# A fused attention kernel: the value products of a tile in two halves, at two places

## The reference

```
scores = jnp.einsum('bhid,bhjd->bhij', q, k) * scale
attn = jax.nn.softmax(scores + causal_mask, axis=-1)
y_softmax = jnp.einsum('bhij,bhjd->bhid', attn, v)
```

## Time and profile before

| | |
|---|---|
| median of 3 runs | 2063.31 us |
| the profiled execution, its time and its span | 2065.87 us, 2064.1 us |
| PE, DVE, ACT, POOL busy, of the span | 88%, 76%, 67%, 56% |
| first stage, attention, third stage (by the places where value products begin and end) | 279, 1610, 175 us |
| value products' matmul records (line 1179) | 2816 + 1792, two for each f32 matmul |
| mean granted clock of TensorE | 0.931 |

### The profile page before, as it was taken

How to read it: one execution, slowest core, us unless ns; L and a number is a source line. 1 busy time by engine, 2 the same in 40 slices (tenths; PEclk the granted TensorE clock), 3 DMA queues, 4 the chain that set the end, 5 groups by cost and what they waited for, 6 DMA issues and landing times. The chain is left out here.

```text
span 2064.1 us, 47119 instructions
## 1 busy us (share of the span) xinstructions
PE 1811.0 (88%) x15280; PEld 706.0 (34%) x15280; DVE 1559.0 (76%) x1712; ACT 1384.5 (67%) x2853; POOL 1147.8 (56%) x1130
## 2 busy tenths in 40 slices
PE   5995589999999899999989999999999999986733
PEld 3452123333334333333343333333333333322622
DVE  5433888888888788887888888888888888501867
ACT  2442158888877788888767888887677887864221
POOL 3102266666666566666665675756576767600535
PEclk9996579999999999999999999999999999997865
DMA  4878131223122312322124214122322121102601
GB/s 127 185 186 208 36 91 57 73 60 85 59 64 78 85 58 85 74 77 66 52 74 95 73 55 99 51 63 68 84 70 84 54 62 59 34 6 74 179 7 75
DMA packets 144582, 163.60 MB, mean 79 GB/s; under 512 B 63440, under 2 KB 91088, under 8 KB 144336
## 3 DMA queue, kind: packets, MB, share of 16 engines
q1 hardware_dynamic: 141952, 158.74, 28.6%
q10 hardware_dynamic: 2384, 1.77, 0.3%
HBM read 122.00 MB, written 38.01 MB: 78 GB/s over the span
## 5 line engine op out<-in xcount | busy, mean ns | idle before, releaser
L1327 DVE TENSOR_REDUCE pmax<-PS 128x2 f32<-128x1024 f32 (+3 forms) x1152 | 1251.1, 1131 | 219.7 <-PE PS L1124 185.1
L1277 ACT ACTIVATE probs<-PS 128x512 f32<-128x512 f32 (+3 forms) x2304 | 1126.5, 567 | 321.6 <-PE PS L1158 231.7
L1158 PE MATMUL PS<-Q_st,K_st 50*128 50x512 f16 (+3 forms) x1408 | 414.8, 363 | 30.2 <-ACT probs L1277 13.6
L1042 POOL TENSOR_TENSOR v_exp<-v_exp,k_rows 128x512 f32<-128x512 f32 x256 | 319.9, 1274 | 64.2 <-DMA v_exp<-qkv_t 63.8
L1124 PE MATMUL PS<-K_st,Q_st 48*128 48x512 f16 (+3 forms) x1408 | 349.7, 360 | 5.3 <-DVE pmax L1327 4.8
L1179 PE MATMUL PS<-probs,V_g 128*17 128x512 f32 (+3 forms) x2816 | 342.8, 560 | 0.0
L1158 PE MATMUL PS<-Q_st,K_first 50*128 50x512 f16 (+3 forms) x896 | 275.4, 382 | 20.2 <-issue 7.2
L1124 PE MATMUL PS<-K_first,Q_st 48*128 48x512 f16 (+2 forms) x896 | 239.8, 413 | 52.1 <-DVE pmax L1327 37.1
L1075 POOL TENSOR_TENSOR state<-ends,q_rows 128x516 f32<-128x516 f32 x256 | 276.1, 1111 | 0.0
L1070 POOL COPY carry<-ends 128x4 f32<-128x4 f32 x64 | 12.1, 189 | 469.4 <-DVE ends L1362 469.4
L1158 PEld LDWEIGHTS PS<-Q_st,K_st 50*128 50x128 f16 x1408 | 110.4, 94 | 406.4 <-ACT probs L1277 326.5
(11 more groups left out here) (163 smaller groups left out, 1584.5 us busy)
## 6 DMA issues: line engine op xcount, KB each, us to landing
v_exp<-qkv_t SPq DMA_DIRECT2D x256, 256.0 KB
qkv_t<-proj SPq DMA_DIRECT2D x24, 512.0 KB, 3.7
qk_parts<-parts SPq DMA_DIRECT2D x16, 512.0 KB, 5.3
Q_st<-qk_parts SPq DMA_DIRECT2D x192, 32.0 KB, 3.4
v_rows<-vaug SPq DMA_DIRECT2D x32, 136.0 KB, 6.6
xin<-x SPq DMA_DIRECT2D x8, 512.0 KB, 6.5
k_rows<-qkv_t SPq DMA_DIRECT2D x16, 256.0 KB, 4.0
q_rows<-qkv_t SPq DMA_DIRECT2D x16, 256.0 KB, 5.0
```

Of the source, the lines that this page charges most:

```text
L1042: pool.tensor_tensor(v_exp[:, n % RING], v_exp[:, n % RING], k_rows[:, b % 2], ALU.mult)\
L1158: mm = pe.matmul(PS[:, bank, 0:CH - r * P], keys[rows, pair, kt * P:(kt + 1) * P], Q_st[rows, c, pair, r * P:CH], start=True, stop=(kt < T ...
L1277: act.activation(probs[:, tile % P_SLOTS, h, 0:CH - r * P], PS[:, step[5], 0:CH - r * P], ACT.Exp, scale=SCORE_SCALE).then_inc(exp_done, 1)
L1327: dve.tensor_reduce(pmax[:, s % 2, pair * TPC + j:GH * TPC:PAIRS * TPC, blk], PS[:, bank:bank + SIDES, 0:width], AX.X, ALU.max).then_inc(m ...
```

## The change

`TILE_ORDER` becomes "SUMMvSSMMRSV". Where the value products of the tile before stood last, with all their columns, there are now two steps: `v` behind the first pair of maxima does columns 0 to 255 of the output (part 0), and `V` at the end does columns 256 to 511 (part 1). The waits (on `exp_done`, and at a chunk's first tile on `out_evacuated` and the values' load) stand before part 0; `values_done` is counted at the end of part 1. Where the mask leaves part 0 no columns (r of 2 or 3), part 0 issues no matmul, only its waits. `PAIR` is 256.

```diff
-TILE_ORDER = "SUMMSSMMRSV"
+TILE_ORDER = "SUMMvSSMMRSV"
...
-    def values():
-        s, kt = pending.pop(0)
-        steps.append(("values", 0, s, kt))
+    def values(part):
+        s, kt = pending[0]
+        steps.append(("values", 0, s, kt, part))
+        if part == 0:
+            return
+        pending.pop(0)
...
-                elif kind == "V":
+                elif kind in "vV":
                     if pending:
-                        values()
+                        values("vV".index(kind))
...
-    values()
+    values(0)
+    values(1)
...
+                        first, end = max(r * P, part * PAIR), (part + 1) * PAIR
+                        if part == 0:
+                            if kt == 0:
+
+                                pe.wait_ge(out_evacuated, g * NCH + s + 1)
+                                if s in FIRST_USE:
+
+                                    pe.wait_ge(loaded["v_" + FIRST_USE[s]], g * 16 + 16)
+
+                            pe.wait_ge(exp_done, g * GH * TILES + GH * (tile + 1) + GH * TILES)
+                        if first >= end:
+                            return
                         for h in range(GH):
-                            mm = pe.matmul(PS[h * VW:h * VW + VN, O_BANK, r * P:CH], v[:, kt, h * VN:(h + 1) * VN],
-                                           probs[:, tile % P_SLOTS, h, 0:CH - r * P],
-                                           start=(kt == 0), stop=(kt == KEY_TILES[s] - 1))
-                        mm.then_inc(values_done, 1)
+                            mm = pe.matmul(PS[h * VW:h * VW + VN, O_BANK, first:end], v[:, kt, h * VN:(h + 1) * VN],
+                                           probs[:, tile % P_SLOTS, h, first - r * P:end - r * P],
+                                           start=(kt == 0 and part == 0), stop=(kt == KEY_TILES[s] - 1))
+                        if part == 1:
+                            mm.then_inc(values_done, 1)
```

More of the change, by code:

```diff
@@ L1162, in scores, with values @@
                         mm.then_inc(scores_ready, 1)
-                    def values(g, s, kt):
+                    def values(g, s, kt, part):
                         c = ORDER[s]
@@ L1168, in values @@
                         r = max(kt - TPC * c, 0)
[L1169 to L1174, removed]
                         v = V_first if s < FIRST_USERS and kt < FIRST * TPC else V_g
-                        pe.wait_ge(exp_done, g * GH * TILES + GH * (tile + 1) + GH * TILES)
-                        for h in range(GH):
-                            mm = pe.matmul(PS[h * VW:h * VW + VN, O_BANK, r * P:CH], v[:, kt, h * VN:(h + 1) * VN],
-                                           probs[:, tile % P_SLOTS, h, 0:CH - r * P],
-                                           start=(kt == 0), stop=(kt == KEY_TILES[s] - 1))
-                        mm.then_inc(values_done, 1)
+                        first, end = max(r * P, part * PAIR), (part + 1) * PAIR
[7 more added lines that the diff above has]
+                            return
+                        for h in range(GH):
+                            mm = pe.matmul(PS[h * VW:h * VW + VN, O_BANK, first:end], v[:, kt, h * VN:(h + 1) * VN],
[3 more added lines that the diff above has]
+                            mm.then_inc(values_done, 1)
                     def lag(g, b, part, bank):
@@ L1230, in walk @@
                             elif kind == "values":
-                                values(g, s, step[3])
+                                values(g, s, step[3], step[4])
                             elif kind == "burst":
```

## The result

The changed kernel takes 2151.66 us (median of 4 runs, 2149.99 to 2154.97) against 2067.19 us (4 runs) before: a ratio of 1.041, with a 95% interval of 1.0372 to 1.0448. It is slower by about 84 us; 2155 us and a ratio of 1.044 had been forecast. The spans of the two profiled executions are 2064.1 and 2149.1 us.

The account below looks back on a forecast made before the run. A plain tile was bound by a ScalarE loop of 2.37 us, becoming 2.60 through v. Terms 48 + 11 + 6 + 5 + 21 = 91 us gave 2154, stated as 2155 us (+4.4%), range 2095 to 2190, likeliest case 2125 to 2190.

Parts of the forecast that it names:

- What bounds the kernel now: Plain attention tile: a loop through ScalarE (S0, its exponential, S3, value products, next S0) of 2.37 us closes the 2.38.
- The wait that moves: Plain tile: v waits for the previous tile's fourth exponential with S1, S2, S3 behind it; new loop 2.60 us, chance 0.78.
- plain tiles: Tiles without burst, lag, turn or mask: +0.22 us each, 48 us in three groups, and 11 us in the last.
- PE's own sum: PE's work in a plain tile, without waits, rises by 0.46 to 2.45 us.
- The rival in which PE alone bounds: Plain tiles: no wait in front of v, 2.45 us a tile or less, 2111 us in all; chance 0.09.
- The split at +0.14: Value products on PE: two halves cost 1.12 us where one whole took 0.98.
- The sum of 91 us: Whole kernel: the added terms, 48 + 11 + 6 + 5 + 21 us.
- masked tiles and chunk beginnings: The four tiles at each of 28 chunk boundaries: 0.75 us a chunk, 21 us, with ends of -11 and +52.
- bursts: 16 a group, set by PE: +0.09 us each, 6 us over 64.
- lags and turns: Some 23 tiles a group where an output's turn adds PE work between V and S0: 0.05 us each, 5 us.
- The halves that help: Rival, plain tiles: shorter V brings S0 0.42 us earlier, ScalarE's idle time goes, tile falls to 2.28, 2026 us; chance 0.06.
- The clock: Rival: PE stalls in every tile drop the clock; one tile in ten at half speed adds 140 us, 2295; chance 0.04.

Follow-up runs that it names:

- the control: The kernel before, value products whole and last in the tile, but taken from the tile two before: 2068.92 us, ratio 1.0005.
- the wait alone: The changed kernel with the waits kept at v's place but no matmul there, all 512 columns at the tile's end: 2072.3 us, ratio 1.0016.
- the halves at the end: The changed kernel with v directly in front of V at the tile's end: 2075.98 us, ratio 1.0018.
- the later tile: The changed kernel with both halves taken from the tile two before instead of the tile before: 2092.26 us, ratio 1.0103.
- v behind S1 and S2: The changed kernel with v two places later, behind score products S1 and S2: 2108.03 us, ratio 1.0184.
- the whole early: The kernel before with its whole value products, 512 columns unsplit, moved to v's place: 2339.24 us, ratio 1.1296.
- the cuts at 128 and 384: The changed kernel with v doing the first 128 or 384 columns instead of 256, V the rest: 2094.73 us (1.013) and 2238.33 us (1.0811).

## Why the prediction was right, step by step

- *What bounds the kernel now.* The loop S0, exponential, S3, V, S0 of 2.37 agrees with the tile's 2.38, and the trace before has S3's load waiting in it:

```profile
903.93 0.09 PEld L1158 LDWEIGHTS PS<-Q_st,K_st 50*128 50x128 f16 x1 [0.30 <-ACT probs L1277]
```

  No experiment tests it: the control, the wait alone and the halves at the end all keep 2.38, but they keep this order of steps too. It is a reading of the trace.
- *The wait that moves.* 2.60 forecast. 2.61 is the commonest distance in all four groups, in 50, 50, 51 and 35 of some 78 plain tiles, the last group included, where 2.44 had stood. Shown by the later tile, v behind S1 and S2, the whole early, and the cuts at 128 and 384.
- *PE's own sum.* 2.45 forecast, 2.40 measured. I took 0.32 for the way from a score product to a value product and 0.55 for v's place; they are 0.30 to 0.31 and 0.53 where nothing waits, and a slot is 0.22. The rival in which PE alone bounds would have come out at 2.40, and it did, at 2092 and 2108 us, where I had it at 2111.
- *The split at +0.14.* The amount was right (two times 0.56 against 0.98), its reason was not said: halves that stand together take 0.99, so the 0.14 is not the second set of matmuls but the second trip from score products to value products and back. The two differ in how they use the array's rows and columns and in their type (fp16 and f32); no run tells which of these costs the time.
- *The sum of 91 us.* The trace gained 85.0. From first exponential to first exponential, over all groups, against the forecast: plain tiles 57.8 us (59), masked tiles and chunk beginnings 12.1 (21), bursts 9.7 (6), lags and turns 0.9 (5), the first three tiles of the groups 3.2 (0), the passages from one group to the next -2.0 (0). That is 82 us, 9 less than forecast. The stretch ahead of the first exponential is 4.9 us longer (275.4 to 280.3), and the stage behind the attention 1.7 shorter. The 4.9 is not the change's: in the ten traces of this case the first exponential starts between 274.5 and 280.9 us, at 274.5 with v behind S1 and S2 and at 280.9 in the control, which splits nothing. The mis-sized terms are masked tiles and turns, taken by rule of thumb. That 2155 lies so near 2151.66 is in part luck: the sum is 7 us above the measured 84.5, and the median of the kernel before came out 3.9 us above the 2063.31 that it was added to.
- *The halves that help.* ScalarE's idle time in front of S0 did go, as that rival says. It came back in front of S1, larger: 0.54 for 0.31.
- *The clock.* It did not fall for the new stop in plain tiles as long as maxima stand in them: in the tiles 6 to 107 of all four groups the granted clock is 1.00 throughout, with v some 0.2 us late in each plain tile. It did fall to 0.50 at the beginning of every group and, behind tile 108 of the last group, where there are no more maxima and TensorE stands still for 0.53 to 0.58 us before v, from 1890.2 to 1907.3. There a plain tile takes 3.47 us instead of 2.61:

```profile
1890.16 1.06 PE L1187 MATMUL PS<-probs,V_g 128*17 128x256 f32 x8 [0.57 <-ACT probs L1286]
...
1893.63 1.05 PE L1187 MATMUL PS<-probs,V_g 128*17 128x256 f32 x8
...
1897.10 1.05 PE L1187 MATMUL PS<-probs,V_g 128*17 128x256 f32 x8
```

  But the kernel before has 17.1 us at 0.50 in that stretch too (1826.9 to 1833.7, 1861.0 to 1871.3, the second behind stops of 0.53 and 0.59 us). From the first to the last exponential it is at 0.50 for some 53 us before and 67 after. An estimate from these two: TensorE at half speed loses at most half of the 14 us, so the clock has at most 7 of the 85 us. Read to the letter, the sign "the granted clock leaves 0.99 inside a group" came true in the last group (0.96), but it stood at 0.97 there before the change. The Trainium skill ("TensorE: Matmul & The Clock Gate", "A second HAM failure mode: psum-queue depth-cycling") says that short and frequent idle times between groups of matmuls, with PSUM banks in rotation, can make the clock go down and up. The tiles with maxima go against that; the end of the last group is in line with it, before the change as well as after.

## What to carry to other kernels

Before moving a consumer forward in an in-order queue, write down what stands behind it and who feeds on that: a wait costs nothing until the work behind it and the work that satisfies it form a loop, and then its length and the moved work's add up. A share of 96% busy on the engine did not tell a loop from work; starts to starts in one repeating tile did. Cut work where it stays together; a half that stands by itself among score products cost 0.14 us more here, and by my sum of TensorE's slots it also leaves a score product without the partner that it ran beside. A mean clock over a whole group (0.96) hides a stretch at half speed: look at the stretch.

## What the runs showed of the hardware that was not expected

- Splitting a column-tiled f32 matmul of 512 columns into two of 256 directly behind each other is free to 0.01 us (0.99 against 0.98), loads included; with score products between the halves it costs 0.14.
- The unchanged kernel varies by 1% from run to run with the mean granted clock: 2061.57 us at 0.933 and 2082.09 us at 0.917, among the 19 runs. Differences under some 10 us between single runs here say nothing.
- Where the maxima have run out, behind tile 108 of the last group, the granted clock was at 0.50 for 17 us in the traces before and after, 14 with both halves at the end, 24 in the control, 38 to 56 with v behind S1 and S2, the later tile, the wait alone and both other cuts, and 99 with the whole value products early. In the tiles 6 to 107 of a group it was there for 3.4 us at most. With one trace of each kernel, how much of that is the kernel's and how much the execution's is open.
